# A sandwich of block-sparse attention and feed-forward: SBUF tensors moved by 64 bytes, and products of zeros in the first batch

## What is computed

```python
def attn(x, w_qkv, b_qkv, w_out, b_out):          # 16 heads of 16
    qkv = x @ w_qkv.T + b_qkv
    q, k, v = split(qkv, 3)
    scores = (q / 4) @ k.T + mask                 # 512 x 512 per head; a token sees its own
    out = softmax(scores) @ v                     # block of 128, and block 0 sees and is seen by all
    return out @ w_out.T + b_out
def ffn(h, W1, b1, W2, b2):                       # 256 -> 1024 -> 256
    return relu(h @ W1 + b1) @ W2 + b2
x = x + layernorm(attn(layernorm(x)))
x = x + layernorm(ffn(layernorm(x)))
```

## The kernel before

| tensor | before | changed |
|---|---|---|
| `w_hi`, `w_lo`, `ident` | 0 | 0 |
| `xa`, `x1_hi`, `x1_lo` | 0 | 64 |
| `stack`, half 0 | 0 | 0 |
| `stack`, half 1 | 0 | 64 |
| `qk`, `probs` | 0 | 0 |
| `values` (its rows are 1148 bytes, its blocks 68 bytes apart) | 0 | 64 |
| `o_t`, `max_bias` | 0 | 64 |
| `o_n`, `o2`, `xr`, `x2`, `h_hi`, `h_lo` | 64 | 64 |
| `ya`, `yf`, `h_f`, `x1_old` | 64 | 0 |

## Time and profile before

### The profile page before, as it was taken

The page is one execution under the profiler, slowest core; times in us unless marked ns, Lnnn a source line. Parts: engine busy times, 40 slices in busy tenths (PEclk is TensorE's granted clock), DMA queues, the critical chain, the costliest instruction groups (busy, mean ns, idle before and its releaser), DMA issues. The chain is left out here.

```text
span 2039.5 us, 71012 instructions
## 1 busy us (share of the span) xinstructions
PE 1926.4 (94%) x27904; PEld 1575.7 (77%) x27904; DVE 1511.4 (74%) x2913; ACT 1406.0 (69%) x2343; POOL 741.6 (36%) x910
## 2 busy tenths in 40 slices
PE   5789999999999999999999999999999999999985
PEld 3458888777878877888777788787788887778775
DVE  4687777787777778778777777777777777876731
ACT  1457767777776777776677777677777677776763
POOL 3113333334333334433343433333433333343343
PEclk7799999999999999999999999999999999999997
DMA  5333434433333433333343333343334344333200
GB/s 144 74 70 80 89 77 86 85 76 82 81 81 79 93 79 80 79 81 81 82 85 80 79 77 81 80 94 78 77 77 86 76 87 85 78 81 69 56 28 17
DMA packets 132815, 160.60 MB, mean 79 GB/s; under 512 B 29408, under 2 KB 82400, under 8 KB 132576
## 3 DMA queue, kind: packets, MB, share of 16 engines
q1 hardware_dynamic: 130544, 154.13, 35.7%
q10 hardware_dynamic: 2032, 2.69, 0.4%
HBM read 38.21 MB, written 17.83 MB: 27 GB/s over the span
## 5 line engine op out<-in xcount | busy, mean ns | idle before, releaser
L817 DVE TENSOR_REDUCE max_bias<-p_pair 128x4 f32<-128x1024 f32 (+1 forms) x640 | 772.8, 1222 | 262.0 <-PE p_pair L571 139.8
L742 ACT ACTIVATE probs<-p_pair 128x1024 f32<-128x1024 f32 x640 | 634.8, 1026 | 208.4 <-PE p_pair L568 127.6
L964 POOL TENSOR_TENSOR h_lo<-h_f,h_hi 128x512 fp32r<-128x512 f32 x256 | 329.7, 1288 | 507.5 <-ACT h_hi L774 507.5
L571 PE MATMUL p_pair<-stack 49*128 49x256 f32 (+1 forms) x3072 | 319.6, 306 | 39.5 <-DVE max_bias L817 22.7
L774 ACT ACTIVATE h_f<-p_pair,b_s 128x256 f32<-128x256 f32 x512 | 248.8, 486 | 133.1 <-PE p_pair L598 133.1
L571 PEld LDWEIGHTS p_pair<-stack 49*128 49x128 f32 (+1 forms) x3072 | 226.9, 188 | 126.7 <-DVE max_bias L817 59.8
L598 PE MATMUL p_pair<-w_hi,h_hi 64*128 64x256 f32 x2048 | 309.4, 279 | 5.0 <-ACT h_hi L774 2.5
L598 PE MATMUL p_pair<-x_hi,w_hi 64*128 64x256 f32 (+1 forms) x2560 | 302.1, 306 | 9.6 <-DVE x_lo L827 5.2
L598 PE MATMUL p_pair<-w_hi,h_lo 64*128 64x256 f32 x2048 | 305.7, 275 | 0.0
L598 PE MATMUL p_pair<-w_lo,h_hi 64*128 64x256 f32 x2048 | 305.5, 275 | 0.0
L598 PE MATMUL p_pair<-x_hi,w_lo 64*128 64x256 f32 (+1 forms) x2560 | 297.7, 302 | 0.0
(11 more groups left out here) (81 smaller groups left out, 2792.9 us busy)
## 6 DMA issues: line engine op xcount, KB each, us to landing
stack<-qk SPq DMA_DIRECT2D x1536, 64.0 KB, 2.3
xr<-x SPq DMA_DIRECT2D x32, 512.0 KB, 4.2
out<-yf SPq DMA_DIRECT2D x64, 256.0 KB, 2.2
xa<-x SPq DMA_DIRECT2D x31, 512.0 KB, 3.8
shift_rows<-max_t SPq DMA_DIRECT2D x128, 8.0 KB, 1.4
stack<-shift_rows SPq DMA_DIRECT2D x128, 8.0 KB
probs<-w_qkv_t SPq DMA_DIRECT2D x2, 384.0 KB, 5.5
ya<-w ACTq DMA_DIRECT2D x1, 512.0 KB, 8.2
```

Of the source, the lines that this page charges most:

```text
L571: last = nc.tensor.matmul(dst[:, j, col:col + HALF].rearrange("p (a n) -> p a n", a=2), stack[r, stationary, at, kb * P:(kb + 1) * P], two ...
L742: nc.scalar.activation(probs[:, prob_slot(quad, c), :, :], banks("scores", n)[:, :, :], ACT.Exp, scale=SCALE).then_inc(exp_done, 1)
L817: nc.vector.tensor_reduce(dst, src, axis=AX.X, op=ALU.max, negate=True).then_inc(red_done, 1)
L964: nc.gpsimd.tensor_tensor(h_parts[1][:, m:m + 2, :], h_f[:, n % 2, :, :], h_parts[0][:, m:m + 2, :].bitcast(F32), ALU.subtract).then_inc(h ...
```

## The change

Two things are changed. First, the SBUF tensors are declared in another order, `stack` becomes a part of `stacks`, whose halves are 16 numbers further apart, and the rows of `max_bias` are 16 numbers longer; the table above says where each tensor comes to lie. What is computed, its order and its waits stay as they are.

Second, a tensor `zeros` of 128 by 128 float32 numbers is set by VectorE as its first instruction, TensorE waits for that once, and `keep_busy` issues products of zeros with zeros, 128 columns wide, into the PSUM banks of a job of batch 0: 16 ahead of `x1`, four ahead of each of the two `qk` units, and five ahead of each of the eight `scores_max` jobs with 512 columns (numbers 0, 1, 5, 6, 10, 11, 15 and 16). That makes 64 products, each of them two instructions in float32. They stand behind the wait for the banks and ahead of the job's other waits.

```diff
--- before.py
+++ after.py
@@ -304,6 +304,8 @@
 PRODUCTS = {"max_t": 4, "o_t": 4, "o2": 1, "op": 1, "x2": 1, "f1": 4, "f2": 2, "x1": 1, "qk": 2, "v": 1}
 READ = {"scores_max": 20, "scores": 20, "max_t": 4, "pv": 4, "o_t": 4, "o2": 1, "op": 1, "x2": 1, "f1": 8, "f2": 2,
         "x1": 1, "qk": 4, "v": 1}
+
+IDLE = {"x1": 16, "qk": 4, "scores_max": 5}
 PAIR_OF = {job[:2]: job[3] for job in ORDER["PE"]}
 
 
@@ -344,39 +346,42 @@
         def sem(name):
             return ctx.enter_context(nc.semaphore(name))
 
+
+
         w_hi, w_lo = sb("w_hi", [P, WCOLS], F32R), sb("w_lo", [P, WCOLS], F32R)
         w_parts = (w_hi, w_lo)
         ident = sb("ident", [P, P])
+
+        stacks = sb("stacks", [P, 2, PAIRS * L + 16], F32R)
+        stack = stacks[:, :, 0:PAIRS * L].rearrange("p a (n l) -> p a n l", l=L)
+
+        qk = sb("qk", [P, 2, 4, L], F32R)
+
+        probs = sb("probs", [P, CH + 2, 2, L])
+        x1_old = sb("x1_old", [P, KB, D])
+        h_f = sb("h_f", [P, 2, 2, HALF])
+        yf = sb("yf", [P, KB, D])
+        b2_s = sb("b2_s", [P, D])
+        ya = sb("ya", [P, KB, D])
         bqk_s, b1_s = sb("bqk_s", [P, 4]), sb("b1_s", [P, KF])
-        b2_s = sb("b2_s", [P, D])
-        minus_half, eps = sb("minus_half", [P, KB]), sb("eps", [P, KB])
         xa = sb("xa", [P, KB, D])
         x1_t = [sb(f"x1_{n}", [P, KD, L], F32R) for n in ("hi", "lo")]
-
-
-        qk = sb("qk", [P, 2, 4, L], F32R)
-
-        stack = sb("stack", [P, 2, PAIRS, L], F32R)
-
-        max_bias = sb("max_bias", [P, 2, 4 * KB + D])
+        o_t = sb("o_t", [P, L])
+        o_n = sb("o_n", [P, KB, D])
+        o2_t = [sb(f"o2_{n}", [P, KD, L], F32R) for n in ("hi", "lo")]
+        xr = sb("xr", [P, KB, D])
+        x2_t = [sb(f"x2_{n}", [P, KD, L], F32R) for n in ("hi", "lo")]
+        h_parts = [sb(f"h_{n}", [P, KF, HALF], F32R) for n in ("hi", "lo")]
+
+        max_bias = sb("max_bias", [P, 2, 8 * KB + D])
         neg_max = [max_bias[:, j, 0:4 * KB].rearrange("p (s j k) -> p s j k", s=2, j=2) for j in range(2)]
         bv_s, bo_s = [max_bias[:, j, 4 * KB:4 * KB + D] for j in range(2)]
         max_t = sb("max_t", [4 * KB, P], F32R)
         shift = nc.dram_tensor("shift_rows", [2, 4 * KB, P], F32, kind="Internal").ap()
         values = sb("values", [P, KB, H * VW + 32 - VW])
-
-        probs = sb("probs", [P, CH + 2, 2, L])
-        o_t = sb("o_t", [P, L])
         den = sb("den", [P, 2, 2 * KB])
-        o_n = sb("o_n", [P, KB, D])
-        o2_t = [sb(f"o2_{n}", [P, KD, L], F32R) for n in ("hi", "lo")]
-        ya = sb("ya", [P, KB, D])
-        xr = sb("xr", [P, KB, D])
-        x2_t = [sb(f"x2_{n}", [P, KD, L], F32R) for n in ("hi", "lo")]
-        x1_old = sb("x1_old", [P, KB, D])
-        h_f = sb("h_f", [P, 2, 2, HALF])
-        h_parts = [sb(f"h_{n}", [P, KF, HALF], F32R) for n in ("hi", "lo")]
-        yf = sb("yf", [P, KB, D])
+        minus_half, eps = sb("minus_half", [P, KB]), sb("eps", [P, KB])
+        zeros = sb("zeros", [P, P])
         KINDS = ("ln1", "lny", "ln2", "lnf")
         bn = {n: sb(f"bn_{n}", [P, KB, 6]) for n in KINDS}
         mv = {n: sb(f"mv_{n}", [P, KB, 2]) for n in KINDS}
@@ -410,6 +415,7 @@
         nmr_done = {n: sem(f"s_nmr_{n}") for n in ("lny", "lnf")}
         norm_done = {n: sem(f"s_norm_{n}") for n in KINDS}
         x1_done, x1_kept, final = sem("x1_done"), sem("x1_kept"), sem("final")
+        zeros_set = sem("zeros_set")
         block = ctx.enter_context(nc.Block())
 
 
@@ -600,6 +606,13 @@
                                                     stop=part == 1 and m == addends - 1, skip_group_check=True)
                 return last
 
+            pe.wait_ge(zeros_set, 1)
+
+            def keep_busy(dst, times):
+
+                for _ in range(times):
+                    nc.tensor.matmul(dst[:, 0, 0:P], zeros[:, :], zeros[:, :], start=True, stop=True)
+
             def job(what, n, b):
                 dst = banks(what, n)
                 if opens(what, n):
@@ -608,6 +621,8 @@
                         wait(pe, free[before[0]], before[2], READ[before[0]], reads(*before[:2]))
                 else:
                     wait(pe, first_part[what], b, PRODUCTS[what], n // 2 + 1)
+                if isinstance(b, int) and b == 0:
+                    keep_busy(dst, IDLE.get(what, 0) if opens(what, n) and (what != "scores_max" or n % CH < 2) else 0)
                 if what == "scores_max":
                     quad, c = n // CH, n % CH
                     if c < 2:
@@ -796,6 +811,8 @@
 
         @block.vector
         def _(dve):
+            nc.vector.memset(zeros[:, :], 0.0).then_inc(zeros_set, 1)
+
             def job(what, n, b):
                 half = slice(HB * n, HB * (n + 1))
                 if what == "split_lo":
```

## The result

The changed kernel takes 2051.75 us (median of nine runs, 2049.5 to 2057.55) against 2044.02 us for the kernel before (nine runs beside them, 2036.53 to 2051.53). The ratio is 1.0041, with a 95% interval from 1.0025 to 1.0056: slower by some 8 us. That is within the 1% that I called no change, and inside the range, but on the other side of no change than the 2035 that I forecast. The profiled execution of the changed kernel took 2056.87 us, that of the kernel before 2041.29: the two lie twice as far apart as the medians.

A forecast was written before the change was run, and what follows sets the result against it. TensorE, busy 94% of the span, was taken as the bound after the first 160 us. 2041.3 less 10 for the places and 1 for the zeros gives 2030, or 2035 against the runs' median; range 2010 to 2056 us.

The forecast's parts named there:

- halves of 128 bytes: TensorE matmuls: operands in the same half run near 0.239 us per four, in opposite halves 0.228, `f1` mostly slow.
- `f1`, `f2` and `op` stay as they are: These TensorE parts keep operands 64 bytes apart, so their rates were taken as unchanged.
- The term for `v`: `v` becomes laid out as `op`: 12 fours at 0.240 less 0.230, saving 0.12 us per batch.
- The terms for the scores: New places save 0.16 us per batch in `scores` and 0.05 in `scores_max`.
- The term for `qk`: `qk`, laid as `f1`, saves between nothing and 0.11 us per batch; 0.05 taken.
- its bound: `pv` taken at nothing; if the shift by 64 matters, at most 0.3 us per batch either way, 10 us in all.
- Four fifths let through: Of 12 us saved in TensorE's stream over 32 batches, four fifths, 10 us, reach the end; waits swallow the rest.
- The zeros: Products of zeros in the start-up: exposed cost 4.2 us at full clock, 8.4 at half, against clock gain; -1 us taken.
- the credit of up to 6 us for a faster clock: Start-up: a fuller TensorE raises the clock, giving 4 us in `qk` and 2 in 30 to 60 us.
- The first, places do nothing: Rival: operand places have no effect, only the zeros count; 2045, up to 2055 if the clock stays low; chance 0.20.
- The second, everything becomes fast: Rival: `f1`, `v`, scores and `qk` all get the fast rate, 27 us saved at the end; 2018; chance 0.23.
- the third, slower: Rival: the slow rate spreads by inheritance to `op`, `f2` and `f1`, costing 16 us; 2071 with zeros; chance 0.07.

The follow-up runs named there:

- e_after128: The changed kernel with 128 unused bytes ahead of `xa`, zeros kept; 2047.64 us, ratio 1.0018 to the kernel before.
- e_best1: The kernel before with four pads, putting `v`, `op`, `f1`, `f2` at distance 64 and `qk` at 192, no zeros; 2041.08 us, ratio 0.9977.
- m_sweep: Separate kernel without the computation: long runs of 64-row matmul pairs at eight operand distances; 256 columns took 117 to 120 ns a pair.
- m_entry: The same sweep in runs of 12 pairs, each on a drained TensorE, with a second moving tensor 64 bytes on; 113.3 ns at some 256-column runs.
- e_worst: The kernel before with pads putting `v`, `op`, `f1`, `f2` at distance 192 and `qk` at 64; 2051.88 us, ratio 1.0027.
- e_zeros: The kernel before with all 64 products of zeros, their tensor behind all others so none moves; 2049.82 us, ratio 1.0031.
- e_zeros_sm: The kernel before with only the 40 products of zeros ahead of `scores_max`; 2050.22 us, ratio 1.0024.
- e_layout: The changed kernel without products of zeros (tensor, memset and one wait stay); 2047.4 us, ratio 1.0012 to the kernel before.

## Why the prediction was wrong

**The reading of the two rates as halves of 128 bytes failed.** The rows were read rightly: `v` slow, `op` and `f2` fast, `f1` mostly slow. The rule that I made of them was not. Modulo 256, and with its sign, weights less moving operand, the distance in the kernel before is 128 for `v`, 64 for `op` and `f2` and 192 for `f1`; the change makes it 192, 192, 192 and 64. `f1` has the weights stationary that `op` and `f2` have moving, so the same two places give distance 64 one way and 192 the other, and the sign is needed. My own rows held the hint: with "opposite halves" `f1` had both rates and `op` one.

**"`f1`, `f2` and `op` stay as they are" failed**, and it was the step that turned the layout's term around, forecast at -10 us and measured at +2.5 (-0.4 to +5.5). `o2`, `x2` and `h`, which I took as unmoved, begin at 64 within 256 bytes before and at 192 after, 128 bytes further, which a table of places within 128 can't show. `f1` gained 0.28 us a turn, `f2` lost 0.36 and `op` 0.07. `e_after128` is the evidence that it is their place and not the new order of the tensors.

**The term for `v`**, 0.12 us, came out at 0.04: at distance 192 it mostly settles at 117.8 ns, not 113.3. In `e_best1`, at distance 64, 52 of 58 parts are fast.

**The terms for the scores**, 0.16 and 0.05, came out at nothing: the steadiest pairs of 256 columns (the quickest quarter) take 119 ns before and 120 to 121 after. They are jobs of a few pairs between others, and I read a rate off them that belongs to longer runs. **The term for `qk`**, 0.05, came out at nothing or a little worse: some 232 ns a pair became about 233. With 512 columns a pair is quicker at distances of 0 and 192 alone (`m_sweep`, `m_entry`), and not at 128, where it was, or at 64, where the change puts it. **`pv`** kept its rate (9.2 us a turn before and after) and its bound was not needed.

**Four fifths let through** was too much for work spread like this. `e_best1` and `e_worst` passed a third to two fifths, and by the far ends of their intervals not more than 7.6 of 12 and 8.6 of 16 us. The busy share of 94% let me take TensorE as the bound everywhere, but behind `x1` it waits for VectorE, and that wait swallows 0.48 us in every turn; behind `x2` all of it comes through. The median turn moves the same way: 60.08 us before, 59.97 in `e_best1` and 60.37 in `e_worst`, where the stream moved by 0.4 and 0.5. It can't be read closer than to 0.1 us: it is 60.19 in `e_zeros` and 60.18 in `e_zeros_sm`, whose tensors lie as before and which run nothing more in the loop. The layout's +0.11 us a turn is 3.5 us of stream; what part of it arrives is lost in the noise of the 2.5 measured.

**The zeros**, forecast at -1, cost 6.3 us (3.9 to 9.0). The cost side fits: I had 4.2 to 8.4 for what is exposed. What failed is the credit of up to 6 us for a faster clock, which brought that down to -1. Its 4 us for `qk` did not come with the zeros but with the execution: `scores_max` 0 started 2.8 us sooner in the changed kernel and 0.9 later in `e_zeros`. The clock in 30 to 70 us was higher with the fives ahead of `scores_max`, but with them the first `pv` came later by 2.1 us in the changed kernel, 2.4 in `e_zeros` and 2.9 in `e_zeros_sm`. Where the rest of the 6.3 us arises is not shown: by the `x1` of the fifth batch `e_zeros` is 3.6 us behind.

**The rivals.** The first, places do nothing, fell with `e_best1`; its 2045 to 2055 for the zeros alone is where the time came out, though its ground, that the places do nothing, was wrong. The forecast's range held the 2051.75 only because it was drawn wide enough to take in this rival. The second, everything becomes fast, came true for `f1` alone. Of the third, slower, the mechanism was half right: `f2` and `op` did come out slow, and beyond the point that I named (101 of 108 `f2` parts), but by their own distance and not by what they inherit, and `f1` went the other way, which I had not put into it; so the layout's price was 2.5 us and not the 16 of that rival. The Trainium skill's rule of two independent read ports (page "TensorE: Matmul & The Clock Gate", section "Step-by-step: what each phase is for") says that a weight load takes nothing from the running matmul. The runs have 113.3 against 117.8 ns for pairs of the same shape: where the weights lie in relation to the moving operand does matter, by 4%. Whether it is the weight load that takes the time is not shown.

## What to carry to other kernels

If a stream of matmuls with short weight loads has two rates for one shape, lay out the byte distance of the two operands modulo 256 or more, with its sign and for every operation that shares a tensor, before any of them is moved; then shift a single tensor by pads of 64 bytes, and count the parts at each rate. Of work saved on a busy engine, ask place by place whether a wait stands right behind it: the same half microsecond was worth nothing at one place of the loop and all of itself at another. Matmuls of zeros in a latency-bound stretch belong only where a wait of known length hides all of them: here those that were exposed cost more than the clock gave back. And judge a start-up stretch by several executions, since one trace shows one course of the clock.

## What was not expected of the hardware

- Pairs of 64-row matmuls with 256 columns have two locked rates, 113.3 and 117.8 ns. Only distances 64 and 192 modulo 256 reached the fast one (in the kernels 64 mostly, 192 in a third of the parts or fewer); at 0 and 128 they take 118 to 120 ns. With 512 columns the fast distances are 0 (226.7 ns in long runs) and 192 (228.8), against 232.5 or more. Why two widths differ in this, what at the start of a run picks the rate, and whether distances 256 bytes apart are alike, stays open.
- The granted clock fell for short times in the steady part too, in profiles of every kernel and at different places: before has two such falls between 200 and 1900 us, the changed kernel six, `e_best1` four. A turn with one takes 61.5 to 62.8 us for about 60.1. No pattern by kernel shows (`e_layout`, `e_zeros` and `e_worst` have two each). Four more falls are some 7 of the 15.6 us between the profiled executions of the changed kernel and of the one before, so that these two traces overstate the loss. Some of the spread between executions of one kernel may be that; it was not tried.
- A float32 product of 128 columns over the whole array took 0.26 us at full clock (five from 45.08 to 46.39 us in the changed kernel) and 0.49 at half (31.71 to 34.14), where I had worked out 0.22 and 0.44 from `pv`.
